# Another order of the first units' work on all engines, in a fused adaLN block on one core

## The reference

```python
mod = (_silu(c) @ wmod).reshape(2, 6, 1, -1)
sa, ca, ga, sb, cb, gb = (mod[:, k] for k in range(6))
ga = (2 * (ga >= 0) - 1) * jnp.maximum(jnp.abs(ga), 0.25)      # gb likewise
h = _layernorm(x) * (1 + ca) + sa
Q, K, V = (h @ W.T + b for each of the three)                  # 16 heads of 16
Q, K = elu(Q) + 1, elu(K) + 1
KV = einsum('bshd,bshe->bhde', K, V);  Z = 1 / (Q . K.sum(axis=1) + 1e-6)
x = x + ga * (einsum('bshd,bhde,bsh->bshe', Q, KV, Z) @ Wo.T + bo)
h = _layernorm(x) * (1 + cb) + sb
logits = cos(h, centroids) + h @ w_route.T;  gates = softmax over the top 2
x = x + gb * sum_e gates_e * (gelu(h @ w1_e + b1_e) @ w2_e + b2_e)
```

## Time and profile before

| | us |
|---|---|
| median of 3 runs | 354.59 |
| lowest, highest | 354.36, 356.01 |
| the profiled execution | 354.88 |
| its span in the trace | 353.2 |

### The profile page before, as it was taken

The page is one execution under the profiler, slowest core; times in us unless marked ns, Lnnn a source line. Parts: engine busy times, 40 slices in busy tenths (PEclk is TensorE's granted clock), DMA queues, the critical chain, the costliest instruction groups (busy, mean ns, idle before and its releaser), DMA issues.

```text
span 353.2 us, 7901 instructions
## 1 busy us (share of the span) xinstructions
PE 337.2 (95%) x2487; PEld 316.0 (89%) x2487; DVE 283.2 (80%) x795; ACT 229.7 (65%) x507; POOL 252.2 (71%) x334
## 2 busy tenths in 40 slices
PE   8888999999999997799999999999999999999895
PEld 8666877877888987799999999999999999999895
DVE  4589777657788789998989999898889887886753
ACT  4566778887877755755748558566585585765441
POOL 4348787868977577988879898898899966755210
PEclk9989999999999999999999999999999999999999
DMA  7956510000000033223232232322432333224311
GB/s 262 333 155 182 181 57 0 0 1 2 2 0 1 3 120 122 74 79 119 70 116 90 63 116 90 97 92 62 132 100 65 108 89 105 91 71 141 106 47 59
DMA packets 23998, 31.79 MB, mean 90 GB/s; under 512 B 2310, under 2 KB 14490, under 8 KB 23964
## 3 DMA queue, kind: packets, MB, share of 16 engines
q1 hardware_dynamic: 23524, 31.34, 28.6%
q10 hardware_dynamic: 440, 0.04, 0.1%
HBM read 27.04 MB, written 4.34 MB: 89 GB/s over the span
## 4 chain that ended last, share of the span: by engine, by line
PE 77%; DVE 9%; ACT 6%; POOL 4%; issue 4%; DVEq 0%; POOLq 0%; ACTq 0%
PE bank L867 20%; PE bank L868 20%; PE bank L869 19%; PE bank L875 5%; PE bank L907 4%; PE bank L1048 2%; PE bank L952 2%; PE bank L899 1%; PE bank L1090 1%; ACT tr_f L659 1%; DVE hid_g L1425 1%; POOL rstd L442 1%; ACT e_sb L683 1%; DVE stats L1192 1%; POOL tr_lo L461 1%
## 5 line engine op out<-in xcount | busy, mean ns | idle before, releaser
L805 ACT ACTIVATE bank<-bank,cols_sb 128x256 f32<-128x256 f32 x128 | 51.5, 440 | 49.3 <-PE bank L869 49.1
L867 PE MATMUL bank<-tr_hi,w_hi 128*128 128x256 f32 x256 | 72.7, 284 | 0.0
L869 PE MATMUL bank<-tr_hi,w_lo 128*128 128x256 f32 x256 | 71.6, 280 | 0.0
L868 PE MATMUL bank<-tr_lo,w_hi 128*128 128x256 f32 x256 | 71.6, 280 | 0.0
L867 PE MATMUL bank<-w_hi,hid_pair 128*128 128x256 f32 x252 | 70.8, 281 | 0.0
L868 PE MATMUL bank<-w_lo,hid_pair 128*128 128x256 f32 x252 | 70.6, 280 | 0.0
L869 PE MATMUL bank<-w_hi,hid_pair 128*128 128x256 f32 x252 | 70.6, 280 | 0.0
L552 POOL TENSOR_TENSOR hid_pair<-hid_g,hid_pair 128x512 fp32r<-128x512 f32 x42 | 54.8, 1306 | 4.4 <-ACT hid_pair L812 2.9
L867 PEld LDWEIGHTS bank<-tr_hi,w_hi 128*128 128x128 f32 x256 | 48.5, 189 | 0.3 <-DVE hid_g L1425 0.2
L868 PEld LDWEIGHTS bank<-tr_lo,w_hi 128*128 128x128 f32 x256 | 48.3, 189 | 0.0
L869 PEld LDWEIGHTS bank<-tr_hi,w_lo 128*128 128x128 f32 x256 | 48.2, 188 | 0.0
(11 more groups left out here) (171 smaller groups left out, 910.0 us busy)
## 6 DMA issues: line engine op xcount, KB each, us to landing
g_bc<-g_dram SPq DMA_DIRECT2D x64, 256.0 KB, 3.6
x_sb<-in_x SPq DMA_DIRECT2D x16, 256.0 KB, 3.7
out<-x_sb SPq DMA_DIRECT2D x15, 256.0 KB, 2.3
early<-in_wmod SPq DMA_DIRECT2D x3, 512.0 KB, 6.1
q_sb<-in_w SPq DMA_DIRECT2D x2, 512.0 KB, 6.4
q_sb<-in_w SPq DMA_DIRECT2D x1, 1024.0 KB, 9.4
mod_row<-mod_dram SPq DMA_DIRECT2D x1, 1024.0 KB, 6.3
q_sb<-in_wqkvT SPq DMA_DIRECT2D x2, 256.0 KB, 4.7
```

The costliest lines, as they stand in the source:

```text
L805: last = ac.activation(half, half, ACT.Gelu, bias=b1_sb[:, e:e + 1])
L867: te.matmul(out_ap, l_hi, r_hi, start=start, stop=False, skip_group_check=shared)
L868: te.matmul(out_ap, l_hi, r_lo, start=False, stop=False, skip_group_check=shared)
L869: return te.matmul(out_ap, l_lo, r_hi, start=False, stop=stop, skip_group_check=shared)
```

## The change

On PE the first series of warm-up matmuls has 20 instead of 24; unit 1 is transposed between `qk(0, 0)` and `qk(0, 1)`; each tile's product waits for its own low half; the centroids' sums move behind step 3. The low halves of units 0 to 3 are made in two instructions, a tile each (`IN_HALVES`). ACT copies the second half of the q/k weights' high part, DVE in turn the bias rows' parts. DVE takes unit 1's statistics right behind the modulation columns and two units' statistics in steps 3 and 4. POOL makes the statistics of units 0 to 7 singly (`SINGLE_POWERS`), and of the later ones in pairs behind the low half and the key sum, in odd steps. The splits of weights 0 to 2 go to ACT (behind steps 1 to 3) and POOL (steps 2 to 4). The modulation rows' work on DVE goes in two parts behind steps 1 and 2, b2's split on ACT behind steps 5 to 7 and on DVE behind step 8, the centroids' behind steps 4 and 8 and the routing weights' behind step 9. `add_bo` of units 0 to 7 moves from steps 2 to 9 into steps 6 to 10 and 13 to 15. SP issues all x loads ahead of the bias and modulation rows.

```diff
-WARM = (24, 20)
+WARM = (20, 20)
 N_SMALL = 3
 MOD_ROWS = (0, 3, 1, 2)
+IN_HALVES = 4
+SINGLE_POWERS = 8
+BO_STEPS = (6, 7, 8, 9, 10, 13, 14, 15)
 def adaln_block(nc, x, wqkvT, rows, cols, woT, w1, w2, b2, cT, wmod, out):
     S, E = x.shape
...
+        def weights_ahead(u):
+            return any(u.nth(j) for j in range(2, 5))
...
-            return u if u < SLOTS else SLOTS + (u - SLOTS) // 2
+            return u if u < SINGLE_POWERS else SINGLE_POWERS + (u - SINGLE_POWERS) // 2
+        def lo_calls(u, t=1):
+            k = u.count()
+            return 2 * k + t + 1 if k < IN_HALVES else IN_HALVES + k + 1
         def xk_bank(b):
...
-            for it in range(2, 4):
+            for it in range(2, NU // 2):
                 load_x(it, 0)
                 load_x(it, 1)
...
-            with sp.Fori(4, NU // 2) as it:
-                for h in range(2):
-                    load_x(it, h)
...
                 wait(pool, a_qk, u.count(2, -2))
-                gp.tensor_tensor(tr_lo[:, h, :, :], tr_f[:, h, :, :], tr_hi[:, h, :, :].bitcast(F32), ALU.subtract)\
-                  .then_inc(a_lo, 1)
+                for t in range(2) if u.count() < IN_HALVES else (None,):
+                    tok = slice(None) if t is None else slice(t * P, (t + 1) * P)
+                    gp.tensor_tensor(tr_lo[:, h, :, tok], tr_f[:, h, :, tok], tr_hi[:, h, :, tok].bitcast(F32),
+                                     ALU.subtract).then_inc(a_lo, 1)
+            def split_weights_lo(i):
+                pool.wait_ge(w_hi_end, i + 1)
+                gp.tensor_tensor(weight_rows(i, 1), w_raw[:, i:i + 1, :], weight_rows(i, 0).bitcast(F32), ALU.subtract)\
+                  .then_inc(w_ready, 1)
...
                 if u.nth(UPB + 6):
                     rstd_e(unit(0))
-                if u.nth(0) or u.nth(1):
+                if any(u.nth(j) for j in range(SINGLE_POWERS - 2)):
                     rstd_a(u.plus(2))
-                elif u.plus(2) and not u.h:
-                    rstd_a(u.plus(2), 2)
                 if u.plus(1):
                     split_lo(u.plus(1))
                 if u.plus(-1):
                     add_ksum(u.plus(-1))
+                if u.h and u.plus(3) and not any(u.nth(j) for j in range(SINGLE_POWERS - 3)):
+                    rstd_a(u.plus(3), 2)
+                if weights_ahead(u):
+                    split_weights_lo(u.count(1, -2))
...
-                if u.nth(2):
+                if u.count() in BO_STEPS:
                     pool.wait_ge(bo_got, 16)
-                if u.plus(-2) and not any(u.nth(j) for j in range(UPB + 2, NU)):
-                    add_bo(u.plus(-2))
+                    add_bo(unit(BO_STEPS.index(u.count())))
...
             step_a(u0)
-            step_a(unit(1))
-            normalise_centroids()
-            step_a(unit(2))
-            for u in range(3, NU):
+            for u in range(1, NU):
                 step_a(unit(u))
+                if u == UPB:
+                    normalise_centroids()
...
                 wait(act, a_tp, u.count(1, 1))
-                wait(act, a_lo, u.count(1, -1))
+                if u.plus(-2):
+                    wait(act, a_lo, lo_calls(u.plus(-2)))
...
                 if u.plus(1) and weights_late(u.plus(1)):
-                    cast_weights(u.plus(1))
+                    cast_weights(u.count(1, 1))
+                if weights_ahead(u.plus(1)):
+                    cast_weights(u.count(1, -1))
             u0 = unit(0)
             normalise(u0)
-            act.wait_ge(zero_rows, 1)
-            act.wait_ge(d_bias, 32)
-            ac.activation(bqk_t[32:33, :], bqk_raw[32:33, :], ACT.Copy).then_inc(bqk_step, 1)
-            ac.activation(bqk_r[0:1, :], bqk_raw[0:1, :], ACT.Copy).then_inc(bqk_step, 1)
+            act.wait_ge(d_qk[1], 16)
+            ac.activation(wqk_hi[:, 1, :], wqk_raw[:, 1, :], ACT.Copy).then_inc(qk_hi_end, 1)
             act.wait_ge(modcol_ready, 1)
             modulate(u0, 0)
             act.wait_ge(a_hf, 1)
             ac.activation(tr_hi[:, 0, :, :], tr_f[:, 0, :, :], ACT.Copy).then_inc(a_hi, 1)
-            act.wait_ge(d_small, 16 * N_SMALL)
-            ac.activation(b2_t, b2_raw, ACT.Copy).then_inc(b2_split, 1)
-            act.wait_ge(warm_done, 1)
-            ac.activation(b2_r[0:NE, :], b2_raw, ACT.Copy).then_inc(b2_ready, 1)
-            ac.activation(b2_r[32:32 + NE, :], b2_raw, ACT.Copy).then_inc(b2_ready, 1)
             normalise(u0.plus(1))
...
                 step_a(unit(u))
+                if 5 <= u <= 7:
+                    split_b2_hi(u - 5)
...
-                if t == 0:
-                    wait(pe, a_lo, u.count(1, 1))
+                wait(pe, a_lo, lo_calls(u, t))
                 tok = slice(t * P, (t + 1) * P)
...
-                if u.plus(1) and not u.nth(0):
+                if u.plus(1):
                     tp_a(u.plus(1))
...
                 qk(u, 1)
-                if u.nth(0):
-                    tp_a(u.plus(1))
                 if u.nth(UPB + 5):
...
-            pe.wait_ge(cent_sq_ready, 1)
-            pe.wait_ge(modcol_ready, 1)
-            for c in range(NC):
-                last = te.matmul(bank[0][:, 0:NE], ones_f, cent_sq[:, c, :], start=(c == 0), stop=(c == NC - 1))
-            last.then_inc(cent_done, 1)
+            def sum_centroids():
+                pe.wait_ge(cent_sq_ready, 1)
+                pe.wait_ge(modcol_ready, 1)
+                for c in range(NC):
+                    last = te.matmul(bank[0][:, 0:NE], ones_f, cent_sq[:, c, :], start=(c == 0), stop=(c == NC - 1))
+                last.then_inc(cent_done, 1)
...
                 step_a(unit(u))
+                if u == 3:
+                    sum_centroids()
...
+            dve.wait_ge(zero_rows, 1)
+            dve.wait_ge(d_bias, 32)
+            ve.tensor_copy(bqk_t[32:33, :], bqk_raw[32:33, :]).then_inc(bqk_step, 1)
+            ve.tensor_copy(bqk_r[0:1, :], bqk_raw[0:1, :])
+            dve.wait_ge(bqk_step, 1)
+            TT(bqk_r[32:33, :], bqk_raw[32:33, :], bqk_t[32:33, :].bitcast(F32), ALU.subtract).then_inc(bqk_ready, 1)
             def low_weights(c):
-                dve.wait_ge(qk_step, c + 1)
...
+            stats_a(u0.plus(1))
             dve.wait_ge(d_qk[1], 16)
-            ve.tensor_copy(wqk_hi[:, 1, :], wqk_raw[:, 1, :]).then_inc(qk_step, 1)
+            dve.wait_ge(qk_hi_end, 1)
             low_weights(1)
             dve.wait_ge(a_hi, 1)
-            TT(tr_lo[:, 0, :, :], tr_f[:, 0, :, :], tr_hi[:, 0, :, :].bitcast(F32), ALU.subtract).then_inc(a_lo, 1)
-            dve.wait_ge(bqk_step, 2)
-            TT(bqk_r[32:33, :], bqk_raw[32:33, :], bqk_t[32:33, :].bitcast(F32), ALU.subtract).then_inc(bqk_ready, 1)
-            stats_a(u0.plus(1))
+            for t in range(2):
+                tok = slice(t * P, (t + 1) * P)
+                TT(tr_lo[:, 0, :, tok], tr_f[:, 0, :, tok], tr_hi[:, 0, :, tok].bitcast(F32), ALU.subtract).then_inc(a_lo, 1)
             dve.wait_ge(d_small, 16 * N_SMALL)
             TT(cent_sq[:, :, :], route_raw[:, :, 0:NE], route_raw[:, :, 0:NE], ALU.mult).then_inc(cent_sq_ready, 1)
...
-                i = u.count(1, 0)
-                if isinstance(i, int):
-                    dve.wait_ge(d_w, 48)
-                src = w_raw[:, bass.ds(i, 1), :]
+                i = u.count()
+                dve.wait_ge(d_w, 48)
+                src = w_raw[:, i:i + 1, :]
                 hi = weight_rows(i, 0)
                 if weights_late(u):
-                    wait(dve, w_hi_end, u.count(1, 1) - (UPB + 1))
+                    wait(dve, w_hi_end, 3 + u.count(1, 1) - (UPB + 1))
                 else:
                     ve.tensor_copy(hi, src).then_inc(w_hi_done, 1)
-                    wait(dve, w_hi_done, u.count(1, 1) - 3 * any(u.nth(j) for j in range(UPB + 4, NU)))
+                    wait(dve, w_hi_done, i + 1 - 3 - 3 * (i > UPB + 3))
                 TT(weight_rows(i, 1), src, hi.bitcast(F32), ALU.subtract).then_inc(w_ready, 1)
...
+            def ahead_of_norm(u):
+                if u < 3:
+                    return (u + 3,)
+                return (2 * u, 2 * u + 1) if u < 5 else range(u + 5, min(u + 6, NU))
...
-                if not u.nth(0) and not u.nth(1):
+                if u.plus(-3):
                     split_weights(u)
+                if u.nth(UPB):
+                    dve.wait_ge(w_ready, UPB + 1)
                 if u.nth(NU - 1):
...
-                if u.nth(0) or u.nth(1):
-                    split_weights(u)
...
-                if u.nth(0):
-                    stats_a(unit(3))
-                if u.nth(1):
-                    stats_a(unit(4))
-                if u.plus(4) and not u.nth(0):
-                    stats_a(u.plus(4))
+                for k in ahead_of_norm(u.count()):
+                    stats_a(unit(k))
             stats_a(unit(2))
-            split_b2()
-            step_a(u0)
-            mod_rows()
-            bias_o()
-            clip_centroids()
-            step_a(unit(1))
```

(35 more changed lines are left out.)

5 lines of the change are left out of this document (2 added, 3 removed).

## The result

| | before | after |
|---|---|---|
| median, us | 354.66 (4 executions) | 350.4 (4 executions) |
| lowest, highest | 354.36, 356.01 | 349.02, 352.28 |
| the profiled execution; its span | 354.88; 353.2 | 349.02; 347.3 |

The ratio is 0.988, 95% interval 0.984 to 0.992: faster by 4.3 us, 1.2%.

A forecast was written before the change was run, and what follows sets the result against it. PE, busy 95% of the span, was taken as the bound, with early holes. Gains 0.7 + 4.9 + 1.3 + 0.75 less 1.3 make 6.35 us, from 354.88 to 348.5 us; range 346.5 to 351.9.

The forecast's parts named there:

- late rise of the clock: Rival to the forecast: PE's clock rises later at the start, costing 2.8 us, time 351.3 us; chance 0.15.
- (a): Start: four fewer warm-up matmuls bring the first product sooner, 10.95 instead of 11.68 us; gain 0.7 us.
- (b): Units 0 to 2: earlier unit 1 statistics and transposes close the first hole, K'x(0) at 19.5 us; gain 4.9 us.
- (c): Steps 2 and 3: single statistics on POOL replace the pair and close the second hole; gain 1.3 us.
- (d): Later pairs of statistics stand behind the low half in odd steps, closing three holes; gain 0.75 us.
- (e): POOL late in steps 5 to 12: unit 9's low half 0.4 us, tp_o(0) 0.9 us; loss 1.3 us.
- the two waits: Part of the gain at units 0 to 2: PE's idle times around unit 1's transposes and first product, 2.35 us.
- The 0.6 for the centroids' sums: Part of the gain at units 0 to 2: centroid sums leave the stretch before the first K'x, 0.6 us.
- fall behind for good: Rival: POOL's backlog in the later steps is not paid back, time 350.2 or up to 354.1 us; chance 0.11.
- The slower rival: The low clock outlasts the start, using up the gain at about 18 us, up to 359.7 us; chance 0.06.

The follow-up runs named there:

- experiment 4: Changed kernel with unit 1's statistics and transposes back at their old places: 352.31 us with 20 warm-ups, 351.73 us with 24.
- experiment 1: The changed kernel run again, nothing altered: 350.7 us, ratio 0.9894.
- experiments 2, 7 and 8: Experiment 2 is the changed kernel with 24 instead of 20 first-series warm-up matmuls: 349.2 us; experiment 7 and experiment 8 have their own lines.
- experiment 3: The kernel before with 20 instead of 24 warm-up matmuls, nothing else changed: 354.76 us, ratio 1.0022.
- experiment 6: Changed kernel with 24 warm-ups and statistics in the old order (POOL's pairs in even steps ahead of the low half): 348.79 us.
- experiment 8: Changed kernel, POOL's step-11 pair behind make_prod(1): 349.4 us; with 24 warm-ups 348.33; then DVE weight splits of steps 11-14 moved later 350.99, only 11-13 347.29.
- experiment 7: Changed kernel with 24 warm-ups and POOL's add_bo of step 9 ahead of its pair of statistics: 350.39 us.

## Why the prediction was right

Forecast 348.5 in a range of 346.5 to 351.9; the median came out at 350.4. Sign and range held. The profiled execution follows the sum closely; that the median lies 1.9 us above the forecast is for 1.4 us the start, whose courses the one profile does not show, and for 0.5 the sum's own excess. The range holds the median because it was widened for a late rise of the clock; the fall that the median's executions seem to have was in none of its cases.

| term | predicted | profiled execution | what the runs showed |
|---|---|---|---|
| (a) start | 0.7 | 0.51 | not from the four matmuls; in nine of ten executions 1.2 to 3.3 us slower than the profiled one |
| (b) units 0 to 2 | 4.9 | 5.28 - 0.51 = 4.77 | 2.3 the fallen clock of the execution before, 2.0 unit 1's order (the halves, 0.4, among what is left) |
| (c) steps 2 and 3 | 1.3 | 6.75 - 5.28 = 1.47 | not by single statistics |
| (d) later pairs | 0.75 | 7.34 - 6.75 = 0.59 | the new order of pairs is not needed for it |
| (e) POOL late | -1.3 | -0.27 at unit 9; -1.12 and -1.04 in steps 12, 13 | tp_o(0) by the pair, as said; DVE's wait behind it not seen |
| unforeseen | | +0.94 in steps 10, 11 | 0.55: DVE's copies no longer beside POOL's addition; 0.39 open |
| sum | 6.35 | 5.85 | |

**(a) failed in the step "four fewer, so up to 0.9 us sooner".** 24 warm-ups in the new order gave the first product at 11.07, 20 gave 11.17: with 20 the products behind ran slower, and unit 0's normalisation on ACT, which the sum did not follow, stands close behind them. About half of the 0.51 gained is PE's wait for DVE's low half, 0.27 before: in experiment 4 with 24 the second series starts at 8.79, as before, and the first product comes 0.25 sooner (11.43). The rival's price was right (2.8 predicted, 22.64 - 19.85 = 2.8 measured), its chance of 0.15 was too small: of ten executions of the changed kernel only the one of 349.02 us is as fast as the 349.09 to 349.55 of the kernel with 24. Three, at 351.73 to 352.28, are where the late rise puts them, and one of these was profiled so; six, at 350.2 to 350.83, have a mean granted clock of 0.993 to 0.995, as the profiled executions with a fall to 0.5 have. For those six no trace was taken, so that they are falls is read from time and clock. The Trainium skill (TensorE: Matmul & The Clock Gate, Part 1) names the variation of the release; experiment 1 shows it. That a clock once granted falls again within the start was in neither sum. And 24 make the fall rarer, not impossible: of the 19 executions of four kernels with 24 and this start (experiments 2, 7 and 8, without the version with four splits moved) six have a mean granted clock of 0.988 to 0.995.

**(b) held in its steps.** From first product to K'x(0) 8.55 us were predicted and 19.85 - 11.17 = 8.68 measured; transposes and products queue without a wait. Its parts came as forecast: 2.0 for the two waits (2.35 predicted) by experiment 4, and 2.3 for the low clock ("some 2 us"), the difference of 13.45 and 11.12 in experiment 3. The 0.6 for the centroids' sums does not show: at a kept clock the old stretch with them (11.12) is 0.2 us longer than experiment 4's without. But the 2.3 belong to an execution whose clock fell. One that keeps it loses most of them again to the wait for unit 2's low half, so how (b) and (c) divide their sum hangs on the one profile.

**(c) was right in size, for the profiled execution, and wrong in cause.** "Single statistics on POOL replace the pair": with the pair back, K'x(2) came at the same distance (experiment 6). What the rows already showed was POOL waiting 1.03 us for DVE at the pair; the statement should have started from that wait. What closed the hole is argued in experiment 6, not shown. The same run takes (d) away from the reordered pairs.

**(e) was right for tp_o(0)** (0.91 measured, 0.9 predicted) and for unit 9 (0.29, 0.4), and missed that `make_prod(1)` stands in the same queue behind the pair: the step that named who waits for the moved pair stopped at the first one, qz(0). Its bound of 3.0 us took the second loss in. The gain in steps 10 and 11 covered it by chance. POOL did not fall behind for good: from 45 to 95 us PE waits for it twice, 0.29 and 0.91 us.

**The slower rival** needed a low clock to about 18 us. The longest at the start lasted to about 14, in experiment 1.

## What to carry to other kernels

Work that fills time ahead of the first product may be what keeps the clock up rather than waste: the order of the units and the length of the warm-up have to be changed apart, and such a start needs several executions, since one profile shows one course of it. When a block is moved in a queue, list every instruction behind it and who waits for each, not the first alone. A stretch at a low clock can hide a wait that comes up once the clock is kept. Before a hole is put down to the long instruction in front of it, read what that instruction itself had waited for.

## What the runs showed of the hardware

**The start takes three courses.** With the clock granted in good time and kept, K'x(0) stood at 19.82 to 20.29 us in the new order; with a late rise at 22.64; with an early rise and a fall at 21.04 and 21.16. The fall came at 8 to 9 us and lasted to 11.5 to 12, at a granted clock of 0.50, in five of the thirteen profiled executions other than the first of the kernel before, two of these with 24 warm-ups. In those two the first series took 4.64 and 4.84 us, in two that kept the clock 4.37 and 4.38, in four more that kept it 5.25 to 5.49. Just before, PE had stood 0.48 to 0.61 us for ACT's normalisation in three of the falls, 0.95 in one and not at all in one, but also 0.63 in an execution that kept the clock. Later falls were seen too: 0.66 from 20 to 25 us in the kernel before, 0.50 from 109 to 112 in experiment 8. What decides stays open.

**The granted clock column does not show the late rise:** it stands at 1.00 while matmuls of 256 columns take 0.225 us each. Only their pace tells.

**DVE's instructions stand still beside POOL's:** with a POOL instruction of 128x512 (1.29 to 1.32 us) running, two copies of 128x4 took 1.26 us instead of 0.23, a cast of 128x256 1.27 instead of 0.23, and the subtraction behind it 1.38 instead of 0.43. Another place for POOL's addition made the copies 1.03 us longer (experiment 7).
